# Storing q and k once per slot, and loading each stack with one DMA

## Chip, cores and metric

The kernel runs on one core of a Trainium2 chip. The metric is the device time of one execution in microseconds (us).

## What is computed

A decoder layer over x of shape (4, 1024, 256): self-attention with a positional bias, cross-attention to a short context, and a mixture of experts, each followed by a residual sum and a layer norm. The change touches the first of the three:

```python
def _L0_attn_ref(x, Wqkv, Wout, Wpos, coeffs):
    ...
    pos_bias = jnp.einsum('ijf,hf->hij', pos_feat, Wpos)
    qkv = jnp.einsum('bsd,ed->bse', x, Wqkv)
    q, k, v = jnp.split(qkv, 3, axis=-1)
    ...
    logits = jnp.einsum('bihd,bjhd->bhij', q, k) * scale + pos_bias[None]
    attn = jax.nn.softmax(logits, axis=-1)
    out = jnp.einsum('bhij,bjhd->bihd', attn, v).reshape(B, S, D)
    return jnp.einsum('bsd,ed->bse', out, Wout)
x = _layernorm(x + _L0_attn_ref(x, ...), axis=-1)
x = _layernorm(x + _L0_xattn_ref(x, ctx_768, mask_BxS_bk0, ...), axis=-1)
x = _layernorm(x + _L0_ffn_ref(x, ...), axis=-1)
```

There are 4 batch rows (B) of 1024 positions (S), together 4096 tokens (T), and 16 heads of 16 dimensions (H, HD).

## The kernel before

The program is a sequence of blocks; in each one every engine has its own instruction list, and semaphores order them. A DMA is issued from the list of one engine, here nearly always SyncE (SP), and its semaphore rises by 16 when it has landed. Lists go on only when a wait (`wait_ge`) is met, so a DMA behind a wait on SP waits too.

`position_tables` makes two lines of the bias and stores them (`pt_line`, and `pt_factor`, which is 16 partitions of 8 KB, to one contiguous piece of DRAM).

`project_qkv` walks over 8 chunks (NCH) of 512 tokens (CH). The scores need q and k in more than bf16's accuracy, so each is split in three bf16 parts: hi (ScalarE, L265), mid (ScalarE, L256, of the rest that VectorE makes at L283) and lo (GpSimd, L306). A chunk has four units u of 128 rows, two of q and two of k, and every unit has one buffer `parts[u]` for its three parts. TensorE makes the unit (L229), ScalarE casts hi after a wait for all stores of the same unit in the chunk before (`unit_stored[u]`, count `per_unit[u]`), and SP's function `store` writes part by part to the DRAM scratch tensors `qstack` and `kstack` (L178), for q also the norms (L182), then v (L187, to `vpad`), then loads x of the chunk after next (L195). The stores of one chunk are thus in one order in one list: for u in 0 to 3 hi, mid, lo. The last two chunks are written out behind the loop. The block ends with `kmax` (L199) and the setup of cross-attention's constants (`cross_setup_pe`, `cross_setup_dve`, `cross_setup_pool`); a new block starts when all engines are through.

A stack in DRAM has 3 x 16 rows (dimension within the head, part) for each of 8 heads, twice, and one row of norms; a row is T elements.

`self_attention` computes 16 groups m (4 head groups of 4 heads, 4 batch rows). For the matmul each head has 97 rows in SBUF: six slots of 16 (SLOTS), which pair the parts of q and k so that the six products of the largest parts add up in one matmul, and one row for the norm and the shift:

```python
Q_PARTS = (0, 0, 0, 1, 1, 2)
K_PARTS = (0, 1, 2, 0, 1, 0)
```

`load_slots` (L325) issues one DMA for each slot, 16 partitions of 4 x 2 KB, so that a part that is in several slots is read several times. SP's `load(m)` issues the six of q, the norm row (L389), the six of k, and v (L391): 14 DMAs on one semaphore, `loaded[m % 2]`; q, k and v have two buffers. At the start SP issues k_max, load(0), the bias strips and factors of head group 0 (L120, L126; 3.84 and 1.92 MB), load(1) and the bias of head group 1; afterwards load(m + 2) when group m is done. Each group has 16 steps (STEPS) over 8 key tiles and 2 halves. A step makes scores of four heads on TensorE (L446), adds the strips on VectorE (L494) or, for some, takes exp on ScalarE and multiplies by the factors on GpSimd (L536), and multiplies with v (L458).

`exact_attention` repeats the attention with exact maxima. It is one large `if` on a flag that the kernel computes, and loads q and k with `load_slots` too.

Of the kernel before, what the change touches and what calls it, by code (L numbers as in the profile page):

```python
# [9 lines left out]
BF16 = mybir.dt.bfloat16  # L10
# [7 lines left out]
P = 128  # L18
B, S, D = 4, 1024, 256
T = B * S  # L20
# [2 lines left out]
HG, HPG = 4, 4  # L23
SLOTS = 6
ROWS = SLOTS * HD
PARTS = 3
NORM_ROW = PARTS * HD
CH = 512
NCH = T // CH
JT = S // P  # L30
# [98 lines left out]
def project_qkv(nc, io, cc, cs):  # L129


    with ExitStack() as ctx:
# [25 lines left out]
        v_stored = [sem(f"v_stored{i}") for i in range(2)]  # L158
        kmax_steps = sem("kmax_steps")
        kmax_stored = sem("kmax_stored")  # L160
        per_unit = [16 * (PARTS + 1), 16 * (PARTS + 1), 16 * PARTS, 16 * PARTS]
        block = ctx.enter_context(nc.Block())

        xT = io["xT"].rearrange("(k p) t -> p k t", p=P)
# [1 line left out]
        @block.sync  # L166
        def _(sp):
            sp.dma_start(members[:, :], io["members"]).then_inc(w_loaded, 16)
            sp.dma_start(w[:, :, :], io["wqkvT"].rearrange("(k p) e -> p k e", p=P)).then_inc(w_loaded, 16)
            for i in range(2):  # L170
                sp.dma_start(x[i][:, :, :], xT[:, :, i * CH:(i + 1) * CH]).then_inc(x_loaded[i], 16)

            def store(c, i):
                for u in range(4):
                    dst = (io["qstack"] if u < 2 else io["kstack"])[u % 2]
                    for part, ready in ((0, hi_done), (1, mid_done), (2, lo_done)):
                        sp.wait_ge(ready, 4 * c + u + 1)
                        sp.dma_start(dst[part * P:(part + 1) * P, bass.ts(c, CH)],  # L178
                                     parts[u][:, part, :]).then_inc(unit_stored[u], 16)
                    if u < 2:  # L180
                        sp.wait_ge(root_done, 2 * c + u + 1)
                        sp.dma_start(dst[NORM_ROW * 8:NORM_ROW * 8 + 8, bass.ts(c, CH)],  # L182
                                     norms[u][:, :]).then_inc(unit_stored[u], 16)
                for n in range(2):
                    sp.wait_ge(v_copied, 1 + 2 * c + n + 1)
                    rows = io["vpad"][bass.ds(c * CH + n * 2 * P, 2 * P), :]
                    sp.dma_start(rows.rearrange("(t p) e -> p t e", p=P),  # L187
                                 v_out[n][:, :, :, :].rearrange("p t h e -> p t (h e)")).then_inc(v_stored[n], 16)

            with sp.Fori(0, NCH // 2 - 1) as pair:  # L190
                for i in range(2):
                    c0 = 2 * pair
                    store(c0 + i, i)

                    sp.dma_start(x[i][:, :, :], xT[:, :, bass.ts(c0 + i + 2, CH)]).then_inc(x_loaded[i], 16)  # L195
            for i in range(2):
                store(NCH - 2 + i, i)
            sp.wait_ge(kmax_steps, 5)
            sp.dma_start(io["kmax"], k_max[:, 3:4]).then_inc(kmax_stored, 16)  # L199
            sp.wait_ge(kmax_stored, 16)  # L200
            for u in range(4):
                sp.wait_ge(unit_stored[u], 1 + per_unit[u] * NCH)
            for n in range(2):
                sp.wait_ge(v_stored[n], 1 + 16 * NCH)
# [108 lines left out]
            cross_setup_pool(nc, pool, cs)  # L313


def part_rows(stack, hg, b, row, n):

    return bass.AP(stack.tensor, (hg // 2) * ((NORM_ROW + 1) * 8 * T) + (hg % 2) * (4 * T) + b * S + row * 8 * T,
                   [[8 * T, n], [T, HPG], [1, S]])


def load_slots(eng, stack, rows, parts, hg, b, done):

    for slot, part in enumerate(parts):
        eng.dma_start(rows[slot * HD:(slot + 1) * HD, :, :], part_rows(stack, hg, b, part * HD, HD)).then_inc(done, 16)  # L325


BY_FACTOR = (0, 2, 3, 5, 6)
NSTEP = HG * B * STEPS

# [16 lines left out]
def self_attention(nc, io, cc):  # L347


    with ExitStack() as ctx:  # L350
# [28 lines left out]

        vsrc = io["vpad"].rearrange("(b j p) (g c) -> b g p j c", j=JT, p=P, c=P)  # L380

        @block.sync
        def _(sp):
            def load(m):
                hg, b, i = m // B, m % B, m % 2
                if m >= 2:
                    sp.wait_ge(pv_done, STEPS * (m - 1))
                load_slots(sp, io["qstack"], q[i], Q_PARTS, hg, b, loaded[i])
                sp.dma_start(q[i][ROWS:ROWS + 1, :, :], part_rows(io["qstack"], hg, b, NORM_ROW, 1)).then_inc(loaded[i], 16)  # L389
                load_slots(sp, io["kstack"], k[i], K_PARTS, hg, b, loaded[i])  # L390
                sp.dma_start(v[i][:, :, :], vsrc[b, hg]).then_inc(loaded[i], 16)  # L391

            def load_bias(hg):
                if hg >= 2:
                    sp.wait_ge(pv_done, B * STEPS * (hg - 1))
                load_strips(sp, io, strips[hg % 2], hg).then_inc(strips_loaded[hg % 2], 16)
                load_factors(sp, io, factors[hg % 2], hg).then_inc(factors_loaded[hg % 2], 16)

            sp.dma_start(k_max[:, :], io["kmax"]).then_inc(kmax_loaded, 16)
            load(0)  # L400
            load_bias(0)
            load(1)
            load_bias(1)
            for n in range(NSTEP // JT):
                sp.wait_ge(o_copied, n + 1)
                hg, column = n // (IH * B), n % (IH * B)
                sp.dma_start(io["oT"][hg, :, column * CH:(column + 1) * CH], o_out[n % 2][:, :]).then_inc(o_stored[n % 2], 16)
                if n % IH == IH - 1 and n // IH + 2 < HG * B:
                    load(n // IH + 2)
                if hg == HG - 1 and n % IH == IH - 1 and column // IH < B - 1:  # L410
                    b = column // IH
                    for i in range(2):
                        sp.wait_ge(o_stored[i], 16 * (n + 1) // 2)
                    sp.dma_start(cc["den"][:, b, :], den_rows(io, b)).then_inc(cc["den_loaded"], 16)
                    sp.wait_ge(cc["rec_done"], b + 1)
                    sp.dma_start(rec_rows(io, b), cc["rec"][:, b, :]).then_inc(cc["rec_stored"], 16)
                if n == NSTEP // JT - 2:
                    sp.wait_ge(cc["rec_stored"], 16 * (B - 1))
                    load_outputs(sp, io, cc["oc0"], cc["recb0"], 0, cc["oc0_loaded"])
                    load_residual(sp, io, cc["x10"], 0, cc["x10_loaded"])  # L420
                if n % (IH * B) == IH * B - 1 and hg + 2 < HG:
                    load_bias(hg + 2)
            for i in range(2):
                sp.wait_ge(o_stored[i], 16 * NSTEP // JT // 2)

        @block.tensor
        def _(pe):
            pe.wait_ge(shift_set, 2 * HPG)

            def scores(s):  # L430
                m, ih, jt = s // STEPS, (s // JT) % IH, s % JT
                if s % STEPS == 0:
                    pe.wait_ge(loaded[m % 2], 16 * (2 * SLOTS + 2) * (m // 2 + 1))
                for half in range(2):
                    if is_factor(s, half):
                        into, ready = ps_factor, factor_scores
# [766 lines left out]
def exact_attention(nc, io, cc, x2_all, logits):  # L1203
# [3 lines left out]
    with ExitStack() as ctx:  # L1207
# [67 lines left out]
        x2T = xT  # L1275
        block = ctx.enter_context(nc.Block())

        @block.sync
        def _(sp):
            needed = sp.value_load(flag[0:1, 0:1], min_val=0, max_val=1)  # L1280
            with sp.If(needed > 0):
                sp.sem_inc(pv_done, 1)
                with sp.Fori(0, HG) as hg:
                    sp.wait_ge(pv_done, 1 + hg * (B * STEPS))
                    load_strips(sp, io, strips, hg).then_inc(strips_loaded, 16)
                    with sp.Fori(0, B) as b:
                        g = hg * B + b
                        sp.wait_ge(pv_done, 1 + g * STEPS)
                        load_slots(sp, io["qstack"], q, Q_PARTS, hg, b, loaded)
                        load_slots(sp, io["kstack"], k, K_PARTS, hg, b, loaded)  # L1290
                        sp.dma_start(v[:, :, :], io["vpad"].rearrange("(b j p) (g c) -> b g p j c", j=JT, p=P, c=P)[b, hg]
                                     ).then_inc(loaded, 16)
                        sp.wait_ge(shift_ready, g + 1)
                        for n in range(SPLIT):
                            sp.dma_start(q[ROWS + n:ROWS + n + 1, :, :].rearrange("p h s -> p (h s)"),
                                         shift_parts[:, n, :]).then_inc(shift_loaded, 16)
                        for ih in range(IH):
                            sp.wait_ge(o_copied, 1 + IH * g + ih + 1)
                            sp.dma_start(io["oT"][hg, :, bass.ds(b * S + ih * CH, CH)], o_out[:, :]).then_inc(o_stored, 16)
# [12 lines left out]
        def _(pe):  # L1312
            needed = pe.value_load(flag[0:1, 0:1], min_val=0, max_val=1)
            with pe.If(needed > 0):
# [1 line left out]
                    pe.sem_inc(free, 1)  # L1316
                pe.wait_ge(ones_set, 1)
                with pe.Fori(0, HG * B) as g:
                    pe.wait_ge(loaded, 16 * (2 * SLOTS + 1) * g + 16 * (2 * SLOTS + 1))
                    for n in range(NM):  # L1320
                        h, it = n // JT, n % JT
                        pe.wait_ge(maxed, 1 + NM * g + n)
# [785 lines left out]
def decoder_layer(nc, io):  # L2108

    def scratch(name, shape, dt=F32):  # L2110
        io[name] = nc.dram_tensor(name, shape, dt).ap()

    scratch("line", [H, 2 * S])
    scratch("factor_line", [H, 2 * S])
    scratch("qstack", [2, (PARTS * HD + 1) * 8, T], BF16)
    scratch("kstack", [2, (PARTS * HD + 1) * 8, T], BF16)
    scratch("vpad", [T, H * 32])
    scratch("kmax", [P, 1])
    scratch("oT", [HG, P, T])
# [99 lines left out]
```

## Time and profile before

| | |
|---|---|
| time, median of 3 runs | 1598.85 us (1594.77 to 1599.28) |
| the profiled execution | 1594.77 us |
| its span in the profile | 1593.0 us |
| TensorE busy | 1337.5 us (84%) |
| VectorE, ScalarE, GpSimd busy | 887.2, 793.9, 655.4 us |
| DMA moved | 163.45 MB, 108380 packets |

The span is from the first to the last instruction on the core. Times in rows count from the start of the span. Busy shares are averages over stages that have different limits, so they say little alone. The first attention block starts at 168 us, and its last score matmuls are at 704 us; the experts take most of the time from 1010 to 1480 us. The DMA share is the mean busy share of the core's 16 DMA engines; it is modelled from packets and can come out a little over 1.

### The profile page before, as it was taken

Reading aid. Unit: us, or ns where it says so; the run is one execution under the profiler, and the core shown is the slowest. Engines: PE = TensorE matmul, PEld = TensorE weight load, DVE = VectorE, ACT = ScalarE, POOL = GpSimd, SP = SyncE. Lnnn points to the kernel's source line nnn. Section 1 sums busy time; section 2 is a strip of 40 time slices with the busy share of each in tenths; the row PEclk is TensorE's granted clock in tenths of the full one; section 3 lists DMA queues with packets and bytes.
Section 4 is the critical chain, followed back from the end, with each engine's and each line's share of the span. In section 5 each row is a group of like instructions: output and inputs, shape, how many; then the busy total and the mean of one; then the engine's idle time right before and its main releaser. Section 6 shows DMA issues by size and latency. Waiting matters only on the chain. (4 is left out here: it accounts for less than half of the span.)

```text
span 1593.0 us, 20872 instructions
## 1 busy us (share of the span) xinstructions
PE 1337.5 (84%) x6346; PEld 605.4 (38%) x6347; DVE 887.2 (56%) x1325; ACT 793.9 (50%) x911; POOL 655.4 (41%) x449
## 2 busy tenths in 40 slices
PE   3998199999999999976999955989999999999200
PEld 1444022222222222213554534646666666666100
DVE  1344278888888888863445426643444343344355
ACT  1774189999999999972556520012222222222000
POOL 0332077777777777753343311111111111111575
PEclk7999589999999999997989955789999999999655
DMA  3674775565566365423121009511111111111243
GB/s 113 210 237 163 208 201 102 95 168 124 97 133 179 76 96 89 79 63 101 62 80 41 1 7 349 204 51 46 46 43 46 44 44 46 46 44 38 83 134 113
DMA packets 108380, 163.45 MB, mean 103 GB/s; under 512 B 12113, under 2 KB 69110, under 8 KB 107766
## 3 DMA queue, kind: packets, MB, share of 16 engines
q1 hardware_dynamic: 99798, 143.41, 33.7%
q0 software_dynamic: 6528, 17.83, 4.0%
q10 hardware_dynamic: 1984, 1.30, 0.3%
q8 instruction: 40, 0.66, 0.2%
q14 instruction: 30, 0.25, 0.0%
HBM read 114.66 MB, written 47.84 MB: 102 GB/s over the span
## 5 line engine op out<-in xcount | busy, mean ns | idle before, releaser
L494 DVE TENSOR_TENSOR sa_probs<-sa_sum,sa_strips 128x1024 f32<-128x1024 f32 x352 | 413.3, 1219 | 98.9 <-PE sa_sum L446 74.0
L536 POOL TENSOR_TENSOR sa_probs<-sa_probs,sa_factors 128x1024 f32<-128x1024 f32 x160 | 380.9, 2381 | 158.4 <-ACT sa_probs L512 125.7
L518 ACT ACTIVATE sa_probs<-sa_probs 128x1024 f32<-128x1024 f32 (+1 forms) x256 | 341.3, 1373 | 7.9 <-DVE sa_probs L494 7.9
L458 PE MATMUL sa_o<-sa_probs,sa_v 128*32 128x512 f32 x2048 | 274.0, 607 | 3.4 <-POOL sa_probs L536 2.9
L1881 PE MATMUL xp_ps_h<-w,arena 128*128 x576 | 261.8, 597 | 1.2 <-ACT arena L1935 1.1
L446 PE MATMUL sa_sum<-sa_q,sa_k 97*128 97x512 bf16 x704 | 199.4, 387 | 34.6 <-DMA sa_v<-vpad 25.7
L1861 POOL DMA_INDIRECT arena<-x_rows,token_of x72 | 68.4, 950 | 385.2 <-PE xp_ps_x L1873 337.1
L1935 ACT ACTIVATE arena<-xp_ps_x 128x256 f32<-128x256 f32 x72 | 27.6, 383 | 381.2 <-PE xp_ps_x L1873 381.2
L1977 DVE TENSOR_TENSOR arena<-xp_ps_h,ffn_b 128x1024 f32<-128x1024 f32 x72 | 88.2, 1225 | 182.9 <-PE xp_ps_h L1881 182.9
L512 ACT ACTIVATE sa_probs<-sa_factor 128x1024 f32<-128x1024 f32 x160 | 163.1, 1020 | 50.3 <-PE sa_factor L446 50.3
L446 PEld LDWEIGHTS sa_sum<-sa_q,sa_k 97*128 97x128 bf16 x704 | 48.5, 98 | 276.8 <-DVE sa_probs L494 199.5
L1881 PEld LDWEIGHTS xp_ps_h<-w,arena 128*128 128x128 f32 x576 | 110.1, 192 | 110.6 <-issue 107.1
L1897 PE MATMUL xp_ps_y<-w,arena 128*128 x576 | 136.4, 380 | 1.0 <-DVE xp_y L1986 0.8
L1897 PEld LDWEIGHTS xp_ps_y<-w,arena 128*128 128x128 f32 x576 | 103.8, 190 | 12.8 <-issue 1.6
L446 PE MATMUL sa_factor<-sa_q,sa_k 97*128 97x512 bf16 x320 | 96.5, 384 | 0.3 <-ACT sa_probs L512 0.3
L979 ACT ACTIVATE cb_pT<-cb_l,arena 77x1024 f32<-77x1024 f32 x64 | 68.4, 1106 | 31.3 <-PE cb_l L884 30.5
L458 PEld LDWEIGHTS sa_o<-sa_probs,sa_v 128*32 128x32 f32 x2048 | 40.4, 108 | 114.0 <-issue 71.0
L306 POOL TENSOR_TENSOR qp_parts<-qp_rest,qp_parts 128x512 bf16<-128x512 f32 x32 | 36.6, 1156 | 105.9 <-ACT qp_parts L256 105.9
L1979 DVE TENSOR_TENSOR arena<-arena 128x512 f32<-128x512 f32 x72 | 49.8, 692 | 50.6 <-ACT arena L1943 50.6
L229 PE MATMUL qp_ps<-qp_x,qp_w 128*128 128x512 f32 x128 | 63.6, 632 | 16.0 <-DMA qp_x<-xT 16.0
L283 DVE TENSOR_TENSOR qp_rest<-qp_ps,qp_parts 128x512 f32<-128x512 f32 x32 | 22.1, 692 | 61.8 <-ACT qp_squares L266 61.8
L884 PE MATMUL cb_l<-cb_qT,arena 32*77 32x512 f32 x256 | 48.9, 640 | 1.1 <-ACT cb_pT L979 1.0
(208 smaller groups left out, 1417.1 us busy)
## 6 DMA issues: line engine op xcount, KB each, us to landing
sa_strips<-line SPq DMA_DIRECT2D x4, 3840.0 KB, 18.5
sa_q<-qstack SPq DMA_DIRECT2D x96, 128.0 KB
sa_k<-kstack SPq DMA_DIRECT2D x96, 128.0 KB
table_y<-xp_y SPq DMA_DIRECT2D x72, 128.0 KB, 1.7
vpad<-qp_v_out SPq DMA_DIRECT2D x16, 512.0 KB, 3.4
sa_v<-vpad SPq DMA_DIRECT2D x16, 512.0 KB
oT<-sa_o_out SPq DMA_DIRECT2D x32, 256.0 KB, 2.3
sa_factors<-factor_line SPq DMA_DIRECT2D x4, 1920.0 KB, 23.2
```

Source lines behind the costliest of these rows:

```text
L229: last = nc.tensor.matmul(ps_u[u][:, :], w[:, k, u * P:(u + 1) * P], x[i][:, k, :], start=(k == 0), stop=(k == KT - 1))
L446: last = nc.tensor.matmul(into[:, a, :], k[m % 2][:, h, jt * P:(jt + 1) * P], q[m % 2][:, h, ih * CH:(ih + 1) * CH], start=True, stop=True)
L458: last = nc.tensor.matmul(ps_o[n % 2][32 * h:32 * h + 32, :], v[m % 2][:, jt, 32 * h:32 * h + 32], probs[s % RING][:, h, :], start=(jt == ...
L494: nc.vector.tensor_tensor(probs[s % RING][:, 2 * half:2 * half + 2, :], ps_sum[sums_before(s, half) % 2][:, :, :], strips[hg % 2][:, 2 * h ...
L512: nc.scalar.activation(probs[s % RING][:, 2:4, :], ps_factor[:, :, :], ACT.Exp, scale=0.25).then_inc(factor_exp, 1)
L518: nc.scalar.activation(probs[s % RING][:, 0:heads, :], probs[s % RING][:, 0:heads, :], ACT.Exp, scale=0.25).then_inc(exp_done, 1)
L536: nc.gpsimd.tensor_tensor(probs[s % RING][:, 2:4, :], probs[s % RING][:, 2:4, :], factors[hg % 2][:, :, c1 - CH:c1][:, :, ::-1], ALU.mult) ...
L979: nc.scalar.activation(pT[:, head:head + 3:2, :], ps_l[use % 2][:NK, :, :], ACT.Exp, bias=neg_shift[:NK, 0:1], scale=HD ** -0.5).then_inc( ...
L1861: pool.indirect_dma_start(out=x[s % 2][:, :], out_offset=None, in_=io["x2_rows"], in_offset=bass.IndirectOffsetOnAxis(token_of[:, s:s + 1], 0)
L1881: last = nc.tensor.matmul(ps_h[parity % 2][:, n, :], xT[parity % 2][:, k, :], w[:, e, k, :], start=(k == 0), stop=(k == KT - 1))
L1897: last = nc.tensor.matmul(ps_y[:, 0:D], gT[parity % 2][:, k, :], w2[:, e, k, :], start=(k == 0), stop=(k == KH - 1))
L1977: nc.vector.tensor_tensor(h[i][:, :, :], ps_h[i][:, :, :], b13[:, e, :, :], ALU.add).then_inc(biased, 1)
```

## The change

The six slots are laid out in DRAM already. SP stores each part once for every slot that holds it, 24 part stores a chunk in place of 12, and both stacks grow from 49 to 97 rows per head. In exchange, a group's q rows come in one DMA of 96 partitions, its k rows in another, the norm row and v as before: 4 DMAs in place of 14. `load_slots` is gone; `part_rows` becomes `rows_of` inside the blocks. The counts that TensorE and ScalarE wait for are changed to match. In SBUF nothing moves.

```diff
-PARTS = 3
-NORM_ROW = PARTS * HD
+NORM_ROW = ROWS
...
-        per_unit = [16 * (PARTS + 1), 16 * (PARTS + 1), 16 * PARTS, 16 * PARTS]
+        per_unit = [16 * (SLOTS + 1), 16 * (SLOTS + 1), 16 * SLOTS, 16 * SLOTS]
...
+                    which = Q_PARTS if u < 2 else K_PARTS
                     for part, ready in ((0, hi_done), (1, mid_done), (2, lo_done)):
                         sp.wait_ge(ready, 4 * c + u + 1)
-                        sp.dma_start(dst[part * P:(part + 1) * P, bass.ts(c, CH)],
-                                     parts[u][:, part, :]).then_inc(unit_stored[u], 16)
+                        for slot in range(SLOTS):
+                            if which[slot] == part:
+                                sp.dma_start(dst[slot * P:(slot + 1) * P, bass.ts(c, CH)],
+                                             parts[u][:, part, :]).then_inc(unit_stored[u], 16)
...
-def load_slots(eng, stack, rows, parts, hg, b, done):
-
-    for slot, part in enumerate(parts):
-        eng.dma_start(rows[slot * HD:(slot + 1) * HD, :, :], part_rows(stack, hg, b, part * HD, HD)).then_inc(done, 16)
...
+        def rows_of(stack, hg, b, row, n):
+
+            return bass.AP(stack.tensor, (hg // 2) * ((ROWS + 1) * 8 * T) + (hg % 2) * (4 * T) + b * S + row * 8 * T,
+                           [[8 * T, n], [T, HPG], [1, S]])
...
-                load_slots(sp, io["qstack"], q[i], Q_PARTS, hg, b, loaded[i])
-                sp.dma_start(q[i][ROWS:ROWS + 1, :, :], part_rows(io["qstack"], hg, b, NORM_ROW, 1)).then_inc(loaded[i], 16)
-                load_slots(sp, io["kstack"], k[i], K_PARTS, hg, b, loaded[i])
+                sp.dma_start(q[i][0:ROWS, :, :], rows_of(io["qstack"], hg, b, 0, ROWS)).then_inc(loaded[i], 16)
+                sp.dma_start(q[i][ROWS:ROWS + 1, :, :], rows_of(io["qstack"], hg, b, ROWS, 1)).then_inc(loaded[i], 16)
+                sp.dma_start(k[i][0:ROWS, :, :], rows_of(io["kstack"], hg, b, 0, ROWS)).then_inc(loaded[i], 16)
                 sp.dma_start(v[i][:, :, :], vsrc[b, hg]).then_inc(loaded[i], 16)
...
-                    pe.wait_ge(loaded[m % 2], 16 * (2 * SLOTS + 2) * (m // 2 + 1))
+                    pe.wait_ge(loaded[m % 2], 64 * (m // 2 + 1))
```

`exact_attention` gets the same two loads, and the scratch tensors `qstack` and `kstack` go from [2, 392, T] to [2, 776, T].

## Rows read from the trace of the kernel before

**Rows 1.** Windows by stage: us from the start, each engine's busy time, TensorE's granted clock, DMA.
```profile
40.00:146.00 106.00, 98.62 (x288) 47.99 (x286) 42.72 (x65) 76.22 (x126) 36.63 (x32) 1.00 0.68 224
146.00:168.00 22.00, 10.20 (x35) 4.77 (x34) 7.78 (x23) 0.24 (x2) 1.31 (x3) 0.73 0.08 27
...
225.00:704.00 479.00, 477.92 (x2903) 112.86 (x2896) 409.57 (x365) 453.89 (x393) 359.58 (x151) 1.00 0.51 104
```

**Rows 2.** Time line of SP's queue in the projection: start, length, line, DMA, count.
```profile
44.41 0.30 SPq L182 DMA_DIRECT2D qstack<-qp_norms  x1
...
47.68 0.30 SPq L182 DMA_DIRECT2D qstack<-qp_norms  x1
48.15 2.81 SPq L178 DMA_DIRECT2D kstack<-qp_parts  x6
51.15 1.03 SPq L187 DMA_DIRECT2D vpad<-qp_v_out  x2
52.38 0.61 SPq L195 DMA_DIRECT2D qp_x<-xT  x1
53.70 3.54 SPq L178 DMA_DIRECT2D qstack<-qp_parts  x3
...
66.99 3.52 SPq L178 DMA_DIRECT2D qstack<-qp_parts  x3
...
133.40 3.54 SPq L178 DMA_DIRECT2D qstack<-qp_parts  x3
```

**Rows 3.** Time line of the engines in the projection, second chunk.
```profile
49.62 3.60 PE L229 MATMUL qp_ps<-qp_x,qp_w 128*128 128x512 f32 x8
...
53.87 0.60 ACT L265 ACTIVATE qp_parts<-qp_ps 128x512 bf16<-128x512 f32 x1
...
59.23 0.57 ACT L265 ACTIVATE qp_parts<-qp_ps 128x512 bf16<-128x512 f32 x1
```

**Rows 4.** Time line of all engines where attention starts.
```profile
167.51 0.15 DVE L673 TENSOR_SCALAR arena<-cs_top 128x1 f32<-128x1 f32 x1 [7.85 <-POOL cs_top L682]
...
168.34 2.77 SPq L325 DMA_DIRECT2D sa_q<-qstack  x6
...
177.12 6.68 SPq L325 DMA_DIRECT2D sa_q<-qstack  x6
...
184.63 1.01 PE L446 MATMUL sa_sum<-sa_q,sa_k 97*128 97x512 bf16 x2 [25.68 <-DMA sa_v<-vpad]
...
193.86 4.71 DVE L494 TENSOR_TENSOR sa_probs<-sa_sum,sa_strips 128x1024 f32<-128x1024 f32 x4 [20.44 <-DMA sa_strips<-line]
...
200.14 6.99 POOL L536 TENSOR_TENSOR sa_probs<-sa_probs,sa_factors 128x1024 f32<-128x1024 f32 x3 [32.66 <-DMA sa_factors<-factor_line]
```

**Rows 5.** Windows around the first loads, one body group, and the store of pt_factor (25:26).
```profile
170.00:182.00 12.00, 0.00 (x0) 0.00 (x0) 3.30 (x8) 0.00 (x0) 0.00 (x0) 0.50 1.08 137
...
184.00:192.00 8.00, 2.72 (x6) 0.72 (x6) 0.00 (x0) 1.02 (x1) 0.00 (x0) 0.50 1.01 419
192.00:197.00 5.00, 1.76 (x4) 0.41 (x5) 3.14 (x3) 1.06 (x1) 0.00 (x0) 0.50 1.01 418
...
238.00:249.00 11.00, 11.00 (x71) 2.53 (x69) 9.17 (x9) 10.40 (x10) 8.70 (x5) 1.00 0.91 172
...
25.00:26.00 1.00, 0.00 (x0) 0.00 (x0) 0.00 (x0) 0.00 (x0) 0.00 (x0) 0.50 1.03 131
```

**Rows 6.** Windows of the projection: a burst of six part stores, and six whole chunks.
```profile
50.00:51.00 1.00, 1.00 (x4) 0.47 (x3) 1.00 (x2) 0.00 (x0) 0.01 (x1) 1.00 0.80 262
...
53.70:133.40 79.70, 74.48 (x216) 36.47 (x216) 31.99 (x48) 58.50 (x97) 27.47 (x24) 1.00 0.74 240
```

**Rows 7.** DMA issues by tile: queue, count, KB each, median us from issue to landing.
```profile
kstack<-qp_parts SPq DMA_DIRECT2D x48, 128.0 KB, 2.0
qp_x<-xT SPq DMA_DIRECT2D x8, 512.0 KB, 5.3
...
kmax<-qp_k_max SPq DMA_DIRECT2D x1, 0.5 KB, 7.3
```

More of the change, by code:

```diff
@@ L313, in _ @@
             cross_setup_pool(nc, pool, cs)
-def part_rows(stack, hg, b, row, n):
-    return bass.AP(stack.tensor, (hg // 2) * ((NORM_ROW + 1) * 8 * T) + (hg % 2) * (4 * T) + b * S + row * 8 * T,
-                   [[8 * T, n], [T, HPG], [1, S]])
-def load_slots(eng, stack, rows, parts, hg, b, done):
-    for slot, part in enumerate(parts):
-        eng.dma_start(rows[slot * HD:(slot + 1) * HD, :, :], part_rows(stack, hg, b, part * HD, HD)).then_inc(done, 16)
 BY_FACTOR = (0, 2, 3, 5, 6)
@@ L1276, in exact_attention, with rows_of @@
         block = ctx.enter_context(nc.Block())
+        def rows_of(stack, hg, b):
+            return bass.AP(stack.tensor, (hg // 2) * ((ROWS + 1) * 8 * T) + (hg % 2) * (4 * T) + b * S,
+                           [[8 * T, ROWS], [T, HPG], [1, S]])
         @block.sync
@@ L1288, in _ @@
                         sp.wait_ge(pv_done, 1 + g * STEPS)
-                        load_slots(sp, io["qstack"], q, Q_PARTS, hg, b, loaded)
-                        load_slots(sp, io["kstack"], k, K_PARTS, hg, b, loaded)
+                        sp.dma_start(q[0:ROWS, :, :], rows_of(io["qstack"], hg, b)).then_inc(loaded, 16)
+                        sp.dma_start(k[0:ROWS, :, :], rows_of(io["kstack"], hg, b)).then_inc(loaded, 16)
                         sp.dma_start(v[:, :, :], io["vpad"].rearrange("(b j p) (g c) -> b g p j c", j=JT, p=P, c=P)[b, hg]
@@ L1318, in _ @@
                 with pe.Fori(0, HG * B) as g:
-                    pe.wait_ge(loaded, 16 * (2 * SLOTS + 1) * g + 16 * (2 * SLOTS + 1))
+                    pe.wait_ge(loaded, 48 * g + 48)
                     for n in range(NM):
@@ L2114, in decoder_layer @@
     scratch("factor_line", [H, 2 * S])
-    scratch("qstack", [2, (PARTS * HD + 1) * 8, T], BF16)
-    scratch("kstack", [2, (PARTS * HD + 1) * 8, T], BF16)
+    scratch("qstack", [2, (ROWS + 1) * 8, T], BF16)
+    scratch("kstack", [2, (ROWS + 1) * 8, T], BF16)
     scratch("vpad", [T, H * 32])
```

## Prediction

> **What bounds the kernel now.** The busy time by stage comes first, since the diff touches the q/k/v projection (40 to 146 us of the span) and self-attention (168 to 709 us) only. [Rows 1] show the projection at 224 GB/s and a DMA share of 0.68, a gap of 22 us in which the DMAs are idle, and the body of attention with TensorE busy 477.92 of 479 us. In that body nothing that SP does can shorten the time unless it comes late. So two places can pay: the projection, and the start of attention before 207 us.
>
> The projection is read in SP's time line and that of the engines [rows 2, 3]. A chunk takes 13.3 us (53.70 to 66.99; (133.40 - 53.70) / 6 = 13.28). SP issues 17 DMAs in it and then waits: its next store can't go out before ScalarE has cast the next chunk's hi part. TensorE runs ahead of it: it starts the chunk's matmuls at 49.62 [rows 3], before SP has stored all of the chunk before.
>
> The start of attention is read in the time line [rows 4]. Setup ends with the shift at 167.51; SP then issues the first group. TensorE's first score matmul starts at 184.63, having waited for q, k and v; VectorE waits for the strips until 193.86; GpSimd for the factors until 200.14, and the first value matmuls wait for GpSimd. All these transfers stand in one queue, and the windows show it full: share 1.08 and only 137 GB/s while q and k load, 419 GB/s for the strips, 418 for the factors [rows 5]. So a microsecond saved on the first q and k moves the strips, the factors and the whole attention by a microsecond.
>
> **The change: loads.** SP's 14 DMAs per group become 4. The bytes and their places in SBUF are the same. What changes is the shape: each slot load writes 16 partitions, the new one 96. At 16 partitions the rate is 137 GB/s. A store of another kind, 16 partitions of 8 KB into contiguous DRAM (pt_factor), runs at 131 GB/s with a full share too [rows 5]; transfers over 128 partitions run at 419. That the number of partitions sets the rate is therefore my reading. The first q and k are 12 x 131,072 = 1.57 MB; from 170 to 182 us is 12.0 us. For 96 partitions no row exists. Bounds: the 137 GB/s of 16 (nothing gained), and the 419 GB/s of 128 (3.8 us, 8.2 gained). By share of partitions, 96/128 x 419 = 314 GB/s, 5.0 us. I take that: **-7.0 us**. The issue of the twelve slot loads (6 in 2.77 us, so 5.5 us [rows 4]) shrinks too, but it lies under the 12 us of transfer and saves nothing of its own.
>
> The Trainium skill, page SBUF — State Buffer, section "Door 1: The DMA port swizzle", says that partitions 0 to 15 reach 4 of 16 ports (104 GB/s measured there), and 64 hardly more than 32. By its map 96 partitions load the even ports with 8 partitions each and the odd ones with 4, which I estimate at 2.4 us for each of q and k, 4.8 us together. That the trace's 16-partition rate is about a third of the 128-partition one agrees with it.
>
> In the body the same loads take about 11 us of each group, at 172 GB/s and a share of 0.91 [rows 5], and are hidden by TensorE's work; shortened, they give nothing. Without that cover each of the 15 groups after the first would gain some 5 us.
>
> **The change: stores.** To fill six slots in DRAM, SP now stores a hi part of q 3 times, mid twice, lo once; for k likewise 3, 2, 1 (K_PARTS). That is 24 part stores a chunk instead of 12, 12.6 MB more over 8 chunks. Two prices.
>
> *SP's issue.* Back to back, 6 stores take 2.81 us, 0.468 each; a norm store 0.47 (47.68 to 48.15); two v stores 1.23 (51.15 to 52.38); the x load and the loop's turn about 1.0 [rows 2]. A chunk is then 24 x 0.468 + 2 x 0.47 + 1.23 + 1.0 = 14.4 us against 13.3. SP falls behind by 1.1 us a chunk.
>
> *The DMA engines.* While six stores go out, the share is 0.80 [rows 6], so 0.80 x 2.81 / 6 = 0.375 us of full engines each. Now: 0.74 x 13.3 = 9.8 us a chunk; new: 9.8 + 12 x 0.375 = 14.3. Both price a chunk at 14.3 to 14.4, so I take 14.4.
>
> Behind SP's queue stand ScalarE (the hi cast of unit u waits for the stores of unit u of the chunk before), TensorE (x of the chunk after next) and VectorE (v_out). How late may SP be? In chunk 0, the first norm goes out at 44.41; then come 18 part stores, a norm, v and x without a wait: 44.88 + 18 x 0.468 + 0.47 + 1.23 + 1.0 = 56.0, against 53.70 now: 2.3 late at the start of chunk 1, and 2.3 + 5 x 1.1 = 7.8 at that of chunk 6. Unit 3's stores are out 24 x 0.468 + 0.94 = 12.2 us after a chunk's start and land 2.0 us later [rows 7]; the next hi cast of unit 3 starts 59.23 - 53.70 + 13.3 = 18.8 after it: slack 4.6. For unit 1, 6.6 + 2.0 against 53.87 - 53.70 + 13.3 = 13.5: 4.9. For x, issued about 13.4 after the start and landing 5.3 later, TensorE needs it at 49.62 - 53.70 + 2 x 13.3 = 22.5: 3.8, with the lag of chunk 5, 2.3 + 4 x 1.1 = 6.7. So the last chunk's compute is late by 7.8 - 4.6 = 3.2 (stores) or 6.7 - 3.8 = 2.9 (x), together not both. A queue that is now deeper takes some slack; I take **+3.5 us**. Below: if a store costs SP 0.43 or less, the chunk stays near 13.5 and the cost is 0. Above: a chunk of 15.5 us gives 2.3 + 5 x 2.2 - 4.6 = 8.7.
>
> The stores' tail costs nothing itself: SP is through its stores at 56.0 + 7 x 14.4 - 1.0 = 155.8 us; kmax then goes out and takes 7.3 us [rows 7], to 163.1, and setup holds the other engines until 167.51 + 3.5 = 171.0. That cover is 8 us wide; past it each microsecond counts. exact_attention changes too, but the trace has none of its loads: its flag is 0. The larger scratch tensors and the changed wait constants add no instruction.
>
> **Sum.** -7.0 + 3.5 = -3.5 us. The profiled execution took 1594.8 us (span 1593.0 and 1.8 around it): 1591.3. It is the fastest of the three shown, 4.1 under their median of 1598.85; against the median the same sum gives 1595.4. I write 1595. From no change, a measurement here can tell about 0.3%, 4.8 us; the forecast is thus "the same, by a little less".
>
> **Rivals.** *The stores are free (0.22).* SP's 0.468 is partly waiting, or the slack takes all of it: cost 0, gain 7 to 8: 1591 to 1592, faster by 0.45%. For it: the DMA share of 0.80 in a burst leaves room, and [rows 2] hold no row of 24 stores in a row. Against it: loads show the same 0.47 (6 in 2.77 us [rows 4]).
>
> *The projection becomes store-bound beyond the slack (0.16): slower than before.* The mechanism is the DMA queue with ScalarE's hi cast behind it: under an uninterrupted stream of writes a packet takes longer, and SP is held back too, as where its issues of the second group took 6.68 us for 6 in a full queue [rows 4]. It decides from the chunk time: to lose 4.8 us net, the cost must be 11.8 us, so a lag of 16.4 at chunk 6, 2.8 us a chunk, a chunk of 16.1 us. At that, 1604. Against it: a chunk moves 24 x 0.131 MB of parts, 1.05 of v and 0.52 of x, 4.7 MB; in 16.1 us that is 294 GB/s, and the burst of [rows 6] stands for 262 / 0.80 = 328 at full share.
>
> *The load doesn't get faster (0.12).* If not the partitions but the source, rows 64 KB apart in the stack, limits q and k, 96 partitions change nothing: gain 0, cost 3.5: 1602, within 0.3%. Against it is the pt_factor store. The Trainium skill, page DMA: Bandwidth & Descriptors, section "Latency and other measured facts", tells of slow copies at row pitches that are large powers of two, from 512 KiB up; no run here shows such a pitch.
>
> **How the numbers follow.** The forecast itself has 0.50. Its terms run from -8.2 to -5 and from +1 to +6, so 1592 to 1600 on the median; a fifth of it lies beyond 4.8 us of gain. Faster by over 0.3%: 0.10 of the forecast and 0.20 of the free stores, 0.30. Slower: 0.15 of the store-bound case, 0.02 of the unchanged load, 0.01 of the forecast, 0.18. Within: the rest, 0.52. The range reaches from a gain of 8.2 at no cost, set against the profiled run (1586.6, so 1587), to a little beyond the store-bound case (1606).
>
> **What would show it.** In the profile after: (1) SP's first stores of chunks 1 and 7 at 56 and about 142 instead of 53.70 and 133.40, a chunk of 14.4 us, DMA share in the projection 0.95 or more; a wait of ScalarE's cast (hi) or of TensorE for DMAs of about 3.5 us in all; (2) setup's last operation at about 171; (3) q and k loaded in about 5 us at some 300 GB/s, the first score matmul 10 us after SP's first load, not 16; strips and factors at 190 and 197; (4) the body unchanged at 100% TensorE. Wrong it would be if the rate at 96 partitions stays under 200 GB/s, if the chunk reaches 16 us, or if TensorE's clock, 0.50 in the windows of the ramp [rows 5], rises at another point of it than now.

## Result and the profile after

The changed kernel takes 1605.15 us (median of 7 runs, 1601.19 to 1608.46) against 1594.77 for the kernel before on the same chips: ratio 1.0061, 95% interval 1.0039 to 1.0083. It is slower by 9.7 us, where a kernel faster by 3.5 us was forecast.

The windows by stage come first (columns as in [rows 1]; the last lines are one chunk and the load of the first q and k):

```profile
40.00:146.00 106.00, 89.47 (x252) 42.56 (x252) 36.85 (x56) 67.56 (x111) 32.04 (x28) 0.98 0.86 281
146.00:168.00 22.00, 18.55 (x63) 8.53 (x61) 8.13 (x16) 9.49 (x17) 4.95 (x5) 1.00 0.82 273
225.00:704.00 479.00, 477.92 (x2902) 112.82 (x2902) 409.50 (x366) 453.73 (x393) 359.69 (x152) 1.00 0.40 111
89.94:106.46 16.52, 12.72 (x36) 6.00 (x36) 5.24 (x8) 10.35 (x18) 4.58 (x4) 1.00 0.90 294
188.00:190.00 2.00, 0.00 (x0) 0.00 (x0) 1.50 (x4) 0.00 (x0) 0.00 (x0) 0.50 1.02 227
```

The projection now runs on through what was the idle gap: 273 GB/s from 146 to 168 us. The body of attention is as before, TensorE busy 477.92 of 479 us. q and k load at 227 GB/s instead of 137 [rows 5]. A chunk takes 16.5 us here, and the DMA engines' share in it is 0.90, not full.

SP's time line, to be set against [rows 2]:

```profile
39.71 4.00 SPq L180 DMA_DIRECT2D qstack<-qp_parts  x6
...
56.86 3.65 SPq L180 DMA_DIRECT2D qstack<-qp_parts  x6
...
89.94 3.62 SPq L180 DMA_DIRECT2D qstack<-qp_parts  x6
93.82 0.30 SPq L184 DMA_DIRECT2D qstack<-qp_norms  x1
94.38 2.92 SPq L180 DMA_DIRECT2D qstack<-qp_parts  x6
97.55 0.30 SPq L184 DMA_DIRECT2D qstack<-qp_norms  x1
98.02 5.79 SPq L180 DMA_DIRECT2D kstack<-qp_parts  x12
103.99 1.03 SPq L189 DMA_DIRECT2D vpad<-qp_v_out  x2
105.21 0.62 SPq L197 DMA_DIRECT2D qp_x<-xT  x1
106.46 3.30 SPq L180 DMA_DIRECT2D qstack<-qp_parts  x6
...
138.52 3.73 SPq L180 DMA_DIRECT2D qstack<-qp_parts  x6
...
153.59 4.05 SPq L180 DMA_DIRECT2D qstack<-qp_parts  x6
```

From the second chunk SP has hardly a gap: 24 stores, norms, v, x, then at once the next chunk. Five chunks from 56.86 to 138.52 are 16.3 us each; the last begins at 153.59 instead of 133.40 [rows 2]. Then the waits from 40 to 180 us (engine, line, who is waited for; us in total, times, longest):

```profile
PE qp_ps L231 <- DMA qp_x<-xT: 8.8, 5, 2.0
...
ACT qp_parts L267 <- DMA kstack<-qp_parts: 4.4, 5, 1.1
```

Both are DMAs that SP issued late: x of a later chunk, and the stores of a unit whose buffer the next hi cast needs. Before there was no such wait. After one of the waits for x, of 2.0 us, TensorE's granted clock fell for a moment (0.54 on average from 111.0 to 114.5 us), and eight matmuls took 5.37 us instead of 3.60 [rows 3]; SP's list ran on without a pause meanwhile, its chunk from 106.46 taking 15.9 us, so the fall shows nowhere in the chunk.

At the start of attention, to be set against [rows 4]:

```profile
183.55 0.15 DVE L668 TENSOR_SCALAR arena<-cs_top 128x1 f32<-128x1 f32 x1 [10.10 <-POOL cs_top L677]
...
184.38 0.43 SPq L383 DMA_DIRECT2D sa_q<-qstack  x1
...
196.01 1.01 PE L441 MATMUL sa_sum<-sa_q,sa_k 97*128 97x512 bf16 x2 [23.26 <-DMA sa_v<-vpad]
...
210.95 7.01 POOL L531 TENSOR_TENSOR sa_probs<-sa_probs,sa_factors 128x1024 f32<-128x1024 f32 x3 [27.43 <-DMA sa_factors<-factor_line]
```

Setup ends 16.0 us later (183.55 against 167.51). The first score matmul follows SP's first load by 11.6 us, not 16.3, and GpSimd gets its factors 10.8 us later than before. 5 us of the 16 are won back, and the rest stays to the end: attention's last copy out of PSUM is at 719.9 instead of 709.6 us, 10.3 later.

### The profile page after: what moved, and what is told of

Same layout as the page of the kernel before. It is cut to its first block and busy times, and to the rows that moved or that the text cites. A ratio compares the mean times of both kernels' runs of the same rounds, so it can differ in the third digit from the quotient of the medians.

```text
span 1600.1 us, 20916 instructions
## 1 busy us (share of the span) xinstructions
PE 1334.3 (83%) x6346; PEld 605.8 (38%) x6347; DVE 885.2 (55%) x1325; ACT 794.6 (50%) x911; POOL 655.6 (41%) x449
## 5 line engine op out<-in xcount | busy, mean ns | idle before, releaser
L1942 ACT ACTIVATE arena<-arena 128x512 f32<-128x512 f32 x72 | 45.3, 629 | 8.9 <-DVE arena L1976 0.3
## 6 DMA issues: line engine op xcount, KB each, us to landing
sa_strips<-line SPq DMA_DIRECT2D x4, 3840.0 KB, 19.4
```

## Experiments

All were run beside the kernel before. For each, the table shows the measured ratio and what its profile gives for three stretches: from SP's first part store to the last operation on k_max (projection), from there to the end of setup, and on to VectorE's first copy of an attention output (start of attention); all us, rounded one by one. e6 leaves the computation out and has no row.

| kernel | ratio (95%) | projection | setup | start of attention | sum |
|---|---|---|---|---|---|
| before | | 110.0 | 17.5 | 54.0 | 181.6 |
| after | 1.0061 (1.0039 to 1.0083) | 125.2 | 18.7 | 48.3 | 192.1 |
| e1 stores only | 1.0117 (1.0093 to 1.0140) | 125.3 | 19.4 | 54.1 | 198.8 |
| e2 issues only | 1.0103 (1.0077 to 1.0129) | 123.0 | 18.3 | 53.9 | 195.2 |
| e3 bytes only | 0.9999 (0.9983 to 1.0014) | 108.9 | 16.5 | 53.8 | 179.2 |
| e4 repeating stores, new loads | 0.9971 (0.9953 to 0.9989) | 109.7 | 17.8 | 47.3 | 174.7 |
| e5 loads only | 0.9969 (0.9953 to 0.9985) | 109.5 | 16.7 | 52.0 | 178.2 |
| e7 18 issues | 1.0014 (0.9994 to 1.0033) | 114.5 | 18.2 | 48.8 | 181.4 |
| e8 as e4, rows side by side | 0.9958 (0.9937 to 0.9979) | 110.5 | 17.5 | 47.1 | 175.0 |

My theory after the result: SP's issue of DMAs sets the projection's time; the rival: the bytes do, through the DMA queue.

**e1, the stores alone.** The changed stores, with the old twelve loads out of the new stack:

```diff
-                sp.dma_start(q[i][0:ROWS, :, :], rows_of(io["qstack"], hg, b, 0, ROWS)).then_inc(loaded[i], 16)
+                for slot in range(SLOTS):
+                    sp.dma_start(q[i][slot * HD:(slot + 1) * HD, :, :],
+                                 rows_of(io["qstack"], hg, b, slot * HD, HD)).then_inc(loaded[i], 16)
...
```

> The changed kernel's 24 part stores a chunk, but q and k loaded with the old twelve 16-partition DMAs (from the new stack). Both theories of the projection (SP's issue time, or the bytes in the DMA queue) expect a chunk of 16.1 us, the last k_max operation on VectorE at 165 us instead of 150. Load theory (16 partitions are slow): first score matmul 16.3 us after SP's first q load, as before, not 11.6 as after. Total 15 to 16 us over before, ratio 1.010; if the old loads cost nothing more than the new ones it is that of the changed kernel, 1.006.

Measured: 125.3 us of projection, as after, and 54.1 for the start of attention, as before; 1.0117, which is 18.7 us. The loss is all in the stores, and the new loads do win some 6 us of it back. The total is 3 us over what was expected; setup's part, 1.9 us longer than before, is in it.

**e2, the issues without the bytes.** The 12 duplicates store 16 partitions instead of 128:

```diff
-                                sp.dma_start(dst[slot * P:(slot + 1) * P, bass.ts(c, CH)],
-                                             parts[u][:, part, :]).then_inc(unit_stored[u], 16)
+                                n = P if which.index(part) == slot else HD
+                                sp.dma_start(dst[slot * P:slot * P + n, bass.ts(c, CH)],
+                                             parts[u][0:n, part, :]).then_inc(unit_stored[u], 16)
```

> 24 part stores a chunk are issued, but the 12 duplicates store only 16 of 128 partitions into slots that nobody reads; old loads, reading each part's first slot, so the result is unchanged. Issue theory (SP pays about 0.5 us for each store, whatever its size): chunk 16 us, k_max at 165 us, total 15 us over before. Bytes theory: chunk 13.3 us, k_max at 150 us, total as before.

**e3, the bytes without the issues.** One DMA stores a part to all its slots; the source repeats. For even steps the slots are put in another order:

```diff
-Q_PARTS = (0, 0, 0, 1, 1, 2)
-K_PARTS = (0, 1, 2, 0, 1, 0)
+Q_PARTS = (0, 0, 0, 1, 2, 1)
+K_PARTS = (2, 1, 0, 0, 0, 1)
+def repeated(dst, src, slots):
+    n = len(slots)
+    step = slots[1] - slots[0] if n > 1 else 1
+    return (bass.AP(dst.tensor, dst.offset, [list(dst.ap[0]), [step * P * T, n], list(dst.ap[1])]),
+            bass.AP(src.tensor, src.offset, [list(src.ap[0]), [0, n], list(src.ap[1])]))
```

> The same 24 copies a chunk, but 12 DMAs: each part goes to all its slots in one DMA whose source repeats (the slots are reordered so that the steps are even); old loads. Issue theory: SP has room again; only the DMA engines' own 14.3 us a chunk can show: k_max between 150 and 156 us, total 0 to 6 us over before. Bytes theory: chunk 16 us, k_max at 165 us, 15 us over before.

One chunk of each, in SP's time line and as a window. e2:

```profile
89.24 3.62 SPq L181 DMA_DIRECT2D qstack<-qp_parts  x6
...
97.27 5.59 SPq L181 DMA_DIRECT2D kstack<-qp_parts  x12
103.05 1.04 SPq L190 DMA_DIRECT2D vpad<-qp_v_out  x2
104.29 0.60 SPq L198 DMA_DIRECT2D qp_x<-xT  x1
105.52 2.73 SPq L181 DMA_DIRECT2D qstack<-qp_parts  x5
```

```profile
89.24:105.52 16.28, 12.76 (x37) 6.00 (x36) 5.24 (x8) 10.27 (x18) 4.58 (x4) 1.00 0.67 214
```

e3:

```profile
83.42 2.78 SPq L190 DMA_DIRECT2D qstack<-qp_parts  x3
...
90.08 3.97 SPq L190 DMA_DIRECT2D kstack<-qp_parts  x6
94.23 1.18 SPq L198 DMA_DIRECT2D vpad<-qp_v_out  x2
95.61 0.98 SPq L206 DMA_DIRECT2D qp_x<-xT  x1
97.22 2.71 SPq L190 DMA_DIRECT2D qstack<-qp_parts  x3
```

```profile
83.42:97.22 13.80, 12.90 (x38) 6.16 (x37) 5.32 (x8) 10.28 (x17) 5.07 (x5) 1.00 1.05 349
```

e2 moves 214 GB/s at a share of 0.67, no more than the kernel before (224 at 0.68 [rows 1]), and its chunk takes 16.3 us (16.1 on average over five). Its k_max comes at 163.9 us and its total is 16.4 us over before, as the issue theory expected. e3 moves all the bytes, at 349 GB/s and a full share; its chunk takes 13.8 (13.7 on average), its k_max comes at 150.0 us, and its total is that of before. So the number of issues costs the time, and the rival falls. What the bytes can have cost is small: without them the projection is still 13.0 us longer than before (e2), with them 15.3 (e1). e3's projection is no longer than that of before, although its chunk is 0.4 longer and its DMA engines are full: the slack takes that. Its twelve stores are issued in more time than before (6 in 3.97 us), but SP has that room.

**e4, both halves without SP's load.** e3's stores, with the changed kernel's loads.

> As the kernel with 12 repeating store DMAs, with the changed kernel's 96-partition loads. Issue theory: k_max at 150 to 156 us, first score matmul 11.6 us after the first q load (16.3 before): total between 5 us under before and 2 over. Bytes theory: the same time as the changed kernel, 10 us over before.

Measured: 0.9971, 4.6 us under before, 14 under after. The first score matmul comes 10.9 us after the first q load. This is the change as it was meant, and it beats both kernels by a little.

**e5, the loads alone.** Twelve stores as before. The stack is laid out [half, batch row, row, head, S], so that four heads of a row are one run. Three loads fill 48, 32 and 16 partitions: those of q repeat one part, those of k read the parts that follow one another:

```diff
-    for slot, part in enumerate(parts):
-        eng.dma_start(rows[slot * HD:(slot + 1) * HD, :, :], part_rows(stack, hg, b, part * HD, HD)).then_inc(done, 16)
+    first = 0
+    for part, n in enumerate((3, 2, 1)):
+        base = part_rows(stack, hg, b, part * HD if parts is Q_PARTS else 0, HD)
+        step = 0 if parts is Q_PARTS else HD * 8 * S
+        eng.dma_start(rows[first:first + n * HD, :, :].rearrange("p h s -> p (h s)"),
+                      bass.AP(base.tensor, base.offset, [[8 * S, HD], [step, n], [1, HPG * S]])).then_inc(done, 16)
+        first += n * HD
```

> The stores of before (12 a chunk, three parts), and the six q and six k slot loads replaced by three each of 48, 32 and 16 partitions, whose source repeats a row; for this the stacks are laid out with the four heads of a row side by side. Theory (the number of partitions of a transfer sets its rate, 137 GB/s at 16): q and k take between 6.7 us (96 partitions, as after) and 12 us, I expect 8; k_max stays at 150 us, first score matmul 12 to 13 us after the first q load (16.3 before), total 3 to 4 us under before, within what can be told. Rival (the projection's gap to attention, not the loads, moved the start): no change in the 16.3 us.

Measured: 0.9969; first score matmul 13.9 us after the first q load, earlier than the 16.3 of before but 0.9 later than expected. Of the 4.9 us in the total the profile accounts for 2.0 at the start of attention and 1.4 before it; the interval reaches from 2.4 to 7.5, so the rest can't be told from nothing. It gains without one more byte stored.

**e6, the loads' rate by itself.**

```diff
+                    for t, first, n, pitch, src, col in loads:
+                        sp.dma_start(a[t][first:first + n, col, :, :], wide(src, n, pitch)).then_inc(done, 16)
+                    count += 16 * len(loads)
+                    sp.wait_ge(done, count)
```

> Leaves out the whole computation: SP alone loads rows of 4 x 2 KB at 64 KB pitch into SBUF, each group awaited before the next: 12 loads of 16 partitions at 0, 16, ..., 80 as in the kernel before; 12 of 16 partitions all at partition 0; then two loads each of 32, 48, 64, 96, 128 partitions; then two of 96 and two of 48 partitions from rows side by side (8 KB pitch). Partition theory: about 130 GB/s for the first two groups, rising with the count, 96 at 230 as in the changed kernel, 128 at 400, and the same rates with rows side by side. Source theory (rows 64 KB apart are slow): 96 and 48 with rows side by side run at about 400 GB/s.

Windows inside each group (columns: VectorE, GpSimd, clock, DMA share, GB/s), in the order of the groups: 16 partitions at 0, 16, ..., 80 in turn; 16 partitions always at partition 0; then 32, 48, 64, 96, 128; 96 and 48 from rows side by side:

```profile
31.00:38.00 7.00, 0.00 (x0) 0.00 (x0) 1.00 1.08 147
44.00:54.00 10.00, 0.00 (x0) 0.00 (x0) 1.00 1.10 109
59.00:60.00 1.00, 0.00 (x0) 0.00 (x0) 1.00 1.02 229
65.00:66.50 1.50, 0.00 (x0) 0.00 (x0) 1.00 1.00 141
72.00:74.00 2.00, 0.00 (x0) 0.00 (x0) 1.00 1.07 215
80.00:83.00 3.00, 0.00 (x0) 0.00 (x0) 1.00 1.06 235
90.00:92.00 2.00, 0.00 (x0) 0.00 (x0) 1.00 1.04 403
97.00:100.00 3.00, 0.00 (x0) 0.00 (x0) 1.00 1.04 262
105.00:107.00 2.00, 0.00 (x0) 0.00 (x0) 1.00 1.00 143
```

At a full share throughout, the rate goes from 109 to 403 GB/s with the partitions written. The first two groups, expected alike at 130, differ: the same twelve DMAs run at 147 GB/s when they go to six places in turn, as in the kernel (137 [rows 5]), and at 109 when all go to one. So it matters which partitions are written, and not only how many. The loads also grow in bytes with their partitions, but that is not what sets the rate: 48 partitions are more bytes than 32 and slower. Rows side by side change little (96: 262 against 235; 48: 143 against 141), so the source theory falls. The rate doesn't follow the count: 32 partitions load at 229, 48 at 141. The Trainium skill, page SBUF — State Buffer, section "Door 1: The DMA port swizzle", has partitions p and p + 32 on one port; 48 partitions then load four of the ports double and finish with them. The trace agrees in the order (48 slower than 32, and 64 at 215 hardly other than 32 at 229; the page measured 196 against 189) and at 16 partitions (109 here, 104 there), not in the size: 48 partitions in twice the time of 32 would be 172 GB/s, and q and k, 4.8 us by the estimate from this map in the prediction, take 6.7 at 235.

**e7, 18 issues.** q's copies are single DMAs, k's repeat.

> q's 12 part stores a chunk stay single DMAs, k's 12 copies go in 6 repeating DMAs: 18 part stores are issued, the same bytes; 96-partition loads. Issue theory: SP needs 16.2 - 6 x 0.49 = 13.3 us a chunk, just what the other engines need, so a chunk of 13.3 to 14 us and k_max 109 to 113 us after the first store (110.0 before, 125.2 after); total between 5 under before and 1 over. If the cost grew evenly with the number of issues instead of setting in past a point, k_max would come 117 us after the first store and the total be 3 us over before.

Measured: 114.5, over the 113 that I expected at most, and under the 117 of even growth. SP's time line says why:

```profile
55.50 3.73 SPq L191 DMA_DIRECT2D qstack<-qp_parts  x6
...
108.20 3.87 SPq L191 DMA_DIRECT2D kstack<-qp_parts  x6
...
130.43 3.68 SPq L191 DMA_DIRECT2D qstack<-qp_parts  x6
```

A repeating DMA costs SP 3.87 / 6 = 0.65 us to issue by the length of its row, where a plain one costs 5.79 / 12 = 0.48, so the six save 1.9 us and not 2.9, and v and x take longer too behind them (1.14 and 0.96 against 1.03 and 0.61 [rows 2]): a chunk is 15.0 us ((130.43 - 55.50) / 5). SP starts chunk 6 at 130.43 - 40.74 = 89.7 us after its first store (40.74), 9.5 late; with the slack of 4.6 that stands in the prediction this gives 4.9 us, and measured are 4.5.

**e8, rows side by side, with e4's stores.** The layout of e5, q and k by one DMA each.

> The kernel with 12 repeating store DMAs and 96-partition loads, and the four heads of a row side by side in the stack, so that a partition's 8 KB are one run. By the load rates (96 partitions: 246 GB/s at 64 KB pitch, 275 side by side) q and k load in 5.7 to 6.4 us instead of 6.7: first score matmul 10 to 11 us after the first q load, total 5 to 7 us under before, not to be told from the kernel without it.

Measured: 0.9958, 10.8 us to the first score matmul as in e4, and all stretches within 1 us of e4's. It is faster than before; that it is faster than e4 isn't shown.

## Why the prediction was wrong

**The step that failed** is the term "24 x 0.468 + 2 x 0.47 + 1.23 + 1.0 = 14.4 us", SP's work in a chunk. It measured 16.3 on average. The chunk from 89.94 takes 16.5, counted from the start of each row to the start of the next: 3.88 + 3.17 + 5.97 = 13.0 for the parts (11.2 assumed), 1.0 for the norms (0.94), 1.2 for v (1.23), 1.25 for x and the turn (1.0). So the error is nearly all in the parts. I divided the length of a row, 2.81 us for six stores, by six; but the next row starts 3.00 us after it (48.15 to 51.15 [rows 2]), so a store takes 0.50 us of SP's list. That is 0.8 of the 1.8 us. The first burst of a chunk takes 0.7 more than the second, since it waits for mid and lo, and the small gaps before the norms are the rest.

The lag grows with what a chunk is over 13.3: 1.9 us more than assumed made it grow by 3.0 a chunk instead of 1.1, and the first chunk was 3.4 us late instead of 2.3. At chunk 6 SP was 138.52 - 39.71 - 80.15 = 18.7 us late instead of 7.8 (80.15 is the same distance before, from a first store at 39.94 to 120.09), and the projection cost 15.2 us instead of 3.5. A chunk of 16 us is what the prediction itself named as a sign that it was wrong.

**The rest of the chain held.** SP is what falls behind; the hi cast and TensorE's x are what wait for it; the slack: 4.6 was worked out, the two kernels give 18.7 - 15.2 = 3.5 and 9.5 - 4.5 = 5.0. Because of it 18 issues cost 4.5 us and 24 cost 15.2. The stores' tail stayed hidden too, though SP issued kmax at 168.2 us, where 155.8 was worked out: setup lasted until 183.55.

**"Both price a chunk at 14.3 to 14.4"** looked like a confirmation and was none. The DMA engines' price of 14.3 us is in full shares, and so e3 bears it out (13.7 us at a share of 1.04 are 14.2), but a share can pass 1, and the bytes went through in 13.7 us. SP's price was too low. That two estimates agree says nothing when each stands for another resource, and the larger decides.

**The slower rival named the wrong mechanism.** It had the outcome, a chunk of 16.1, but from a full DMA queue in which packets take longer. The share in a chunk was 0.90, and e2 is nearly as slow at 0.67. SP wasn't held back by a full queue either: its stores follow one another at the same distance before and after (3.00 us for six, 5.97 for twelve). That the measured 1605 still lies in the range, whose upper end was set by this rival, is luck and no merit of the forecast's path.

**The loads** were right in kind and mis-sized: 314 GB/s by share of partitions, measured 227 in the kernel and 235 alone; 7.0 us were forecast and the start of attention is 5.7 us shorter (54.0 to 48.3). That the rate hangs on the partitions written is shown (e6), but not that it goes by their share of 128; and faster loads give nothing in the body: its rows are unchanged. Of the 5.7 us, 4.7 lie before the first score matmul. The other 1.0 lies behind it, where TensorE's granted clock rose from 0.50 to 1.00 sooner: about 21 us after that matmul (at 217 us) instead of 23 (at 207). That this is the reason wasn't tested.

**Setup** was taken as fixed and came out 1.2 us longer (18.7 against 17.5). Two of its parts changed. From k_max to VectorE's reduction for cs_top it took 8.4 us instead of 9.5. TensorE's granted clock was 1.00 there (164.9 to 173.3 us), against 0.82 before (150.0 to 159.5); in all the other runs, too, this part took 8.4 us where the clock was 0.99 or 1.00 (e2, e3, e5) and 9.5 where it was 0.78 to 0.83 (e1, e4, e7, e8). Then GpSimd's wait between its reduction of cs_top and the next operation was 9.0 us instead of 6.8; it was 8.6 in e1 and e2, 7.4 in e7, and 6.7 to 7.1 in e3, e4, e5 and e8. It goes with the stores that SP still had to issue when k_max was ready (kmax went out 3.3 us later in the changed kernel, 3.2 and 2.8 in e1 and e2, 1.0 in e7, 0.2 elsewhere). No run was made for it, and the cause is open.

**The sum**: 15.2 - 5.7 + 1.2 = +10.7 by the rounded table (10.5 by its last column), against 9.7 measured (6.2 to 13.2).

## What to carry over

Price a list of issues from the start of one row to the start of the next, gaps and waits included, in a stretch in which it works without a break; and where a stage has slack, know that the loss begins only past it and then repeats in every turn. Copies that have one source belong into one DMA with a repeating source: 12 issues with all the bytes were as fast as the kernel before, 24 with few more bytes cost 16 us. Whether stores issued from a second engine's list would help as well was not tried. Before a load is merged for its count of DMAs, see which partitions it writes: that was the gain here, and only where nothing hid the load.

## What the hardware showed

- SP issues plain part stores of 128 x 1 KB one every 0.50 us, in the kernel before as in the changed one (5.97 us from the start of twelve to the next row). When half of the twelve write only 16 partitions, the twelve take 5.59 us instead of 5.79 (e2): the bytes matter little.
- Stores with a repeating source are issued one every 0.65 to 0.68 us (3.87 us for six in e7). The DMA share was 0.85 in those stretches (108.20 to 112.07 us), so a full queue is not the reason; whether it is the form of the DMA or its two copies on average was not separated.
- A DMA of 48 partitions from partition 0 ran at 141 GB/s, of 32 at 229, of 96 at 235, of 128 at 403, each with the DMA engines' share at 1.00 to 1.07; twelve of 16 partitions ran at 109 to one place and at 147 to six places in turn. A full share says nothing of the bytes that move.
- One queue can hold 349 GB/s of mixed stores and loads for a whole chunk (e3).
